# Half of h's last block in one stationary operand: 17 down products for a tile and not 18

## What is computed

```python
def fp4_quant_dequant(x):            # along the last dim, in blocks of 16
    xb = x.reshape(shape[:-1] + (shape[-1] // BLOCK, BLOCK))
    scale = jnp.maximum(jnp.max(jnp.abs(xb), axis=-1, keepdims=True) / 6.0, 1e-12)
    ...                              # round xb / scale to the FP4 grid, times scale
def fp4_linear(x, w):
    return jnp.einsum('bsk,nk->bsn', fp4_quant_dequant(x), fp4_quant_dequant(w))

x = x + xattn(layernorm(x), ctx)     # 16 heads of 64, 154 context rows
xn = layernorm(x)
h = silu(fp4_linear(xn, w_gate)) * fp4_linear(xn, w_up)    # 704 hidden columns
out = x + fp4_linear(h, w_down)                            # 704 -> 256
```

## Time and profile before

| | us |
|---|---|
| median of 3 runs | 885.43 |
| lowest, highest | 885.17, 888.35 |
| the profiled execution | 887.63 |
| its span, first to last instruction | 885.5 |
| TensorE busy in it | 834.0 (94%) |
| VectorE busy | 709.2 (80%) |
| POOL busy | 539.2 (61%) |
| ScalarE busy | 525.7 (59%) |
| mean granted TensorE clock | 0.988 of 2.4 GHz |

### The profile page before, as it was taken

How to read it: one execution, slowest core, us unless ns; L and a number is a source line. 1 busy time by engine, 2 the same in 40 slices (tenths; PEclk the granted TensorE clock), 3 DMA queues, 4 the chain that set the end, 5 groups by cost and what they waited for, 6 DMA issues and landing times.

```text
span 885.5 us, 19161 instructions
## 1 busy us (share of the span) xinstructions
PE 834.0 (94%) x6278; PEld 805.2 (91%) x6278; DVE 709.2 (80%) x2157; ACT 525.7 (59%) x1878; POOL 539.2 (61%) x810
## 2 busy tenths in 40 slices
PE   4887799999999999999999999999999999999986
PEld 4766789999988999999998999999999999999985
DVE  5659788877877888887877888887778788888887
ACT  4555466666665666667565666666666666666531
POOL 6437766765644666675653766665644577666644
PEclk9889999999999999999999999999999999999999
DMA  8101000001010000001000000000100000000000
GB/s 248 37 25 45 1 20 13 24 14 48 8 37 19 13 26 13 26 13 43 13 31 25 7 24 14 24 14 13 50 7 19 13 14 25 14 19 14 7 7 19
DMA packets 20137, 23.14 MB, mean 26 GB/s; under 512 B 2658, under 2 KB 18250, under 8 KB 20042
## 3 DMA queue, kind: packets, MB, share of 16 engines
q1 hardware_dynamic: 20042, 21.94, 8.2%
HBM read 17.74 MB, written 4.19 MB: 25 GB/s over the span
## 4 chain that ended last, share of the span: by engine, by line
PE 81%; DVE 11%; POOL 3%; issue 2%; ACT 2%; DVEq 0%; POOLq 0%; ACTq 0%
PE ps_g L1246 12%; PE ps_s L1203 11%; PE ps_q L1161 10%; PE ps_t L1213 7%; PE ps_o L1226 7%; PE ps_o L1228 7%; PE ps_o L1227 7%; PE ps_g L1124 3%; PE ps_m L1089 3%; PE ps_m L1260 3%; PE ps_m L1262 2%; PE ps_m L1261 2%; PE ps_q L1124 2%; DVE negmax L884 1%; DVE pT_lo L737 1%
## 5 line engine op out<-in xcount | busy, mean ns | idle before, releaser
L511 POOL TENSOR_TENSOR probs<-probs,rsum 128x308 f32<-128x308 f32 x256 | 179.5, 702 | 244.5 <-DVE rsum L848 244.1
L684 ACT ACTIVATE probs<-ps_s,negmax 128x154 f32<-128x154 f32 x512 | 194.7, 386 | 190.2 <-DVE negmax L884 188.4
L884 DVE TENSOR_REDUCE negmax<-ps_s 128x2 f32<-128x308 f32 x256 | 121.1, 473 | 92.5 <-PE ps_s L1203 91.6
L1226 PE MATMUL ps_o<-B_sb,pT_lo 128*128 128x256 f32 x640 | 180.9, 283 | 0.9 <-DVE x_both L939 0.6
L1228 PE MATMUL ps_o<-B_sb,pT_hi 128*128 128x256 f32 x640 | 180.6, 282 | 0.0
L1227 PE MATMUL ps_o<-B_sb,pT_hi 128*128 128x256 f32 x640 | 180.3, 282 | 0.0
L737 DVE TENSOR_TENSOR pT_lo<-ps_t,pT_hi 128x256 fp32r<-128x256 f32 (+1 forms) x256 | 122.9, 480 | 34.4 <-ACT pT_hi L572 34.0
L1246 PE MATMUL ps_g<-WGU,xqT_hi 128*128 128x352 f32 x504 | 131.8, 343 | 2.0 <-DVE B_sb L737 1.7
L1213 PE MATMUL ps_t<-ident,probs 128*128 128x128 f32 x640 | 112.8, 274 | 15.4 <-DVE pT_lo L737 13.2
L1226 PEld LDWEIGHTS ps_o<-B_sb,pT_lo 128*128 128x128 f32 x640 | 121.1, 189 | 1.4 <-issue 0.8
L1228 PEld LDWEIGHTS ps_o<-B_sb,pT_hi 128*128 128x128 f32 x640 | 121.4, 190 | 0.0
(11 more groups left out here) (228 smaller groups left out, 2213.8 us busy)
## 6 DMA issues: line engine op xcount, KB each, us to landing
xa<-in_x_dram SPq DMA_DIRECT2D x33, 128.0 KB, 2.2
xr<-in_x_dram SPq DMA_DIRECT2D x32, 128.0 KB, 2.0
out_dram<-y_xn SPq DMA_DIRECT2D x30, 128.0 KB, 1.7
W_sb<-in_L_xattn_Wk_dram SPq DMA_DIRECT2D x4, 512.0 KB, 4.6
W_sb<-in_L_xattn_Wv_dram SPq DMA_DIRECT2D x3, 512.0 KB, 3.3
probs<-in_L_xattn_Wq_dram SPq DMA_DIRECT2D x2, 512.0 KB, 8.0
Wo_sb<-in_L_xattn_Wo_dram SPq DMA_DIRECT2D x1, 1024.0 KB, 9.2
VT<-in_L_ffn_w_down_dram SPq DMA_DIRECT2D x2, 352.0 KB, 3.9
```

The source lines that it names most:

```text
L511: pool.tensor_tensor(unit, unit, rsum[:, 2 * u:2 * u + 2].unsqueeze(2) .to_broadcast([P, 2, M]), ALU.mult).then_inc(norm_p, 1)
L684: ins = act.activation(probs[:, h, 0:M], ps_s[k % 2][:, s * M:(s + 1) * M], ACT.Exp, bias=negmax[:, h:h + 1], accum_out=sums[:, h:h + 1])
L884: dve.tensor_reduce(negmax[:, 2 * k:2 * k + 2], ps_s[k % 2][:, 0:UM].rearrange("p (h m) -> p h m", h=2), AX_X, ALU.max, negate=True).then_ ...
L1226: pe.matmul(ps_o[:, 0:C], lo[:, j, :], w[:, 0:C], start=first, stop=False)
```

## The change

The last block of h has only 64 rows that aren't zero. The changed kernel puts the low part of this half block below the high part, in partitions 64 to 127 of hqT[0]'s block 5. WD's block 5 gets the weights' half block twice, in partitions 0 to 63 and 64 to 127. Two matmuls with this operand, one with the weights' low part and one with their high part, then give (high + low) x (high + low), where there were three. For that:

- VectorE's hqT_lo of blocks 3 to 5 becomes two operations: blocks 3 and 4 as before into hqT[1] (128x256), and the half block from partitions 0 to 63 into partitions 64 to 127 of hqT[0] (64x128).
- POOL fills the padding of the w_down chunks with the last 64 columns' rounded values and no longer with zeros: a product of 128x64 between the second and third step of `fp4`, on the same queue. The two memsets and the wait for b_mm go, and TensorE's wait for pad_p with them.
- The three tiles in `finish` keep 18 matmuls with low parts of their own; since WD's padding isn't zero any more, VectorE sets tile 31's padding of h to zero.

```diff
+            def round_stage(c, i):
+                n = RAW_N[c]
+                v, scale = raw[RAW_IN[c]], raw_s[c % 2][:, 0:n // BLOCK]
+                if i == 2 and c >= DOWN:
+
+                    pool.wait_ge(raw_p, 3 * c + 2)
+                    pool.tensor_tensor(v[:, F:FP].rearrange("p (b k) -> p b k", k=BLOCK),
+                                       v[:, F - D:F].rearrange("p (b k) -> p b k", k=BLOCK),
+                                       scale[:, (F - D) // BLOCK:].unsqueeze(2).to_broadcast([P, D // BLOCK, BLOCK]),
+                                       ALU.mult).then_inc(pad_p, 1)
+                    pool.wait_ge(pad_p, c - DOWN + 3)
+                fp4(v[:, 0:n], raw_c[c % 2][:, 0:n], scale, raw_p, 3 * c, (raw_v, 6 * c + 6), (i,))
+
             def round_chunk(c):
-                n = RAW_N[c]
-                fp4(raw[RAW_IN[c]][:, 0:n], raw_c[c % 2][:, 0:n], raw_s[c % 2][:, 0:n // BLOCK], raw_p, 3 * c,
-                    (raw_v, 6 * c + 6))
+                for i in range(3):
+                    round_stage(c, i)
...
-                    if isinstance(t, int) and t == 1 and k == 0:
-
-                        pool.wait_ge(b_mm, B_JOBS)
-                        for c in range(DOWN, CHUNKS):
-                            pool.memset(raw[RAW_IN[c]][:, F:FP], 0.0).then_inc(pad_p, 1)
...
                     if down and k in (5, 6):
                         r = k - 5
-                        lo_part(hqT[1][:, 3 * r:3 * r + 3, :], parts(ps_m, 3), hqT[0][:, 3 * r:3 * r + 3, :],
-                                (hqT_hi, 2 * d + r + 1), hqT_lo)
+                        if r == 0:
+                            lo_part(hqT[1][:, 0:3, :], parts(ps_m, 3), hqT[0][:, 0:3, :], (hqT_hi, 2 * d + 1), hqT_lo)
+                        else:
+                            dve.wait_ge(hqT_hi, 2 * d + 2)
+                            dve.tensor_tensor(hqT[1][:, 3:5, :], parts(ps_m, 2), hqT[0][:, 3:5, :].bitcast(F32), ALU.subtract)
+                            dve.tensor_tensor(hqT[0][D:P, 5, :], ps_m[0:D, 2 * P:3 * P], hqT[0][0:D, 5, :].bitcast(F32),
+                                              ALU.subtract).then_inc(hqT_lo, 1)
...
                 weights_lo(T, PAIRS - 1)
+                dve.memset(hnT[:, F:FP], 0.0).then_inc(ppad_v, 1)
...
                 pe.wait_ge(raw_p, 3 * c + 3)
-                if c == DOWN:
-                    pe.wait_ge(pad_p, 4)
...
-                down_terms(ps_m, *hqT, range(FT)).then_inc(d_mm, 1)
+                down_terms(ps_m, *hqT, range(FT - 1))
+
+                for part in range(2):
+                    ins = pe.matmul(ps_m[:, 0:C], hqT[0][:, FT - 1, :], WD[:, FT - 1, part * C:(part + 1) * C],
+                                    start=False, stop=(part == 1))
+                ins.then_inc(d_mm, 1)
...
                     pe.wait_ge(hd_v, 3)
+                    pe.wait_ge(ppad_v, 2)
...
-                down_product(R, (xqT_lo, S + 1))
+                m_free((xqT_lo, S + 1), (y_v, R + 1))
+                pe.wait_ge(hqT_lo, 2 * R + 2)
+                down_terms(ps_m, *hqT, range(FT)).then_inc(d_mm, 1)
```

## The result

The changed kernel takes 891.37 us (median of 6 runs, 889.26 to 893.52). The kernel before, on the same chips, takes 886.50 (6 runs, 884.94 to 888.35). The ratio is 1.0057, with a 95% interval of 1.0040 to 1.0074: the change costs 4.9 us, between 3.5 and 6.6. The forecast was +4.05 us on 885.43, the median of the three runs known then.

The account below looks back on a forecast made before the run. The prediction took both TensorE and VectorE to be on the path in every tile. Its terms, -3.42 + 6.68 + 0.74 + 0.05 = +4.05 us on a median of 885.43, gave 889.5 us, range 884.0 to 892.0.

Parts of the forecast that it names:

- matmul removed: Down product on TensorE, 29 tiles: one matmul less saves 0.118 us each, 3.42 us in all.
- given back behind the matmul: VectorE's stretch from slot 0's negmax: all 3.42 us counted as arriving, since 0.19 of 0.31 us idle time remain.
- VectorE's pair: Slot 6, hqT_lo split in two: both operations held as in K_lo, +0.30 us a tile, +6.68 us in all.
- w_down's preparation: Weight setup on POOL: two 128x64 products of +0.37 us each, on the path, 0.74 us, between 0 and 1.0.
- tail: Last tiles: VectorE gets a memset of 64 columns, 0.05 us, between 0 and 0.1.
- Rival (b): Slot 6: a write into the other half doesn't hold VectorE, +1.39 in place of 6.68, 884.2 us; chance 0.11.
- Rival (c): Slot 6's second operation: moving between partition halves costs more than K_lo's pair, +0.19 us in 23 tiles, 893.9; chance 0.08.
- Rival (a): Whole kernel: busy shares are right and VectorE's extra time is hidden behind TensorE, 882.8 us; chance 0.06.
- What is late next: Slot 7's transposes start 0.30 us later in 12 tiles, 0.28 in 11; in six tiles idle time takes it.
- A steady pair: Two steady tiles, from product to product, now 45.60 us, would take 0.34 us more.
- the warm-up up to tile 3 moves by more than 1 us: Time up to tile 3: named as one sign that the prediction is wrong.
- The prediction's line between same and slower: Whole time: about 0.5% can be told from no change, 889.9 us; same 0.59, slower 0.38.

Follow-up runs that it names:

- e2: Kernel before with 18 down matmuls and only VectorE's split, second operation writing the other partition half: 892.66 us, ratio 1.0080.
- e4: Kernel before with only the change's w_down preparation on POOL and the tail's memset: 886.32 us, ratio 1.0009.
- e8: The changed kernel run once more, nothing altered: 891.18 us, ratio 1.0045 against the kernel before.
- e3: Kernel before with 18 down matmuls and only VectorE's split, second operation writing the same half it reads: 886.37 us, ratio 1.0014.
- e5: Changed kernel with the 64x128 operation moved to slot 7 behind pT_lo, except in five setup steps: 882.20 us, ratio 0.9950 against the kernel before.
- e7: The kernel before run once more, nothing altered: 885.68 us, ratio 0.9995.
- e6: Kernel before with 17 matmuls, VectorE's operation whole, POOL doubling h's half block, ACT copying the high part: 889.09 us, ratio 1.0021.
- e9: Changed kernel with POOL's addition of the output bias moved from slot 0 to slot 5: 889.2 us, run once.
- e10: Kernel before with 17 down matmuls, VectorE's operation whole, POOL's output bias addition moved from slot 0 to 5: 885.2 us, run once.
- e11: e5 with POOL's addition of the output bias moved from slot 0 to slot 5: 881.93 us, ratio 0.9962 against the kernel before.

## The prediction against the runs, point by point

| term | predicted | measured | from |
|---|---|---|---|
| matmul removed, 29 x 0.118 | -3.42 | -3.42 | start to start in the product |
| given back behind the matmul | 0 | about +0.6 | 19 x 0.034 us of hn<-eh,scales; the middle: 3.52 + 3.30 - 22 x 0.28 |
| VectorE's pair | +6.68 | about +6.4 | 23 x 0.28; e2's rows |
| w_down's preparation | +0.74 | +0.73 | e4's front, one execution |
| tail | +0.05 | not told apart | the changed kernel's own two are 40.98 and 41.61 |
| sum | +4.05 | about +4.3 | timed: +4.9 (3.5 to 6.6) |

- **The matmul.** Price and place were right. The step that was wrong is the sentence that the 0.118 us reaches VectorE's next stretch as long as the idle time before negmax isn't used up. That idle time did remain, 0.17 us where the prediction said 0.19:

```profile
325.56 0.48 DVE L896 TENSOR_REDUCE negmax<-ps_s 128x2 f32<-128x308 f32 x1 [0.17 <-PE ps_s L1214]
```

  But a test for idle time before one operation isn't a test for what comes behind it. 0.7 us later VectorE and POOL meet in an operation that a shift of 0.12 us turns into a wait, and in slot 1 TensorE then waits for the q_lo that stands behind it (the q product starts at 329.00, 0.05 us behind q_lo's end, and 0.19 behind the transposes in front of it where it was 0.15). By the durations it cost some 0.6 of the 3.42 us (0.65 in this trace, 0.46 in e8's); what moving the addition gives back is 0.49 in the 14 undisturbed periods.
- **The split.** Both times were taken from K_lo and came out: second start 0.42 to 0.43 us behind the first, 283 to 286 ns long, negmax 0.32 behind. The pair is 0.74 us and not 0.75, the cost 0.28 and not 0.30: priced about 0.3 us too high over all tiles. The open question, whether the output alone holds, is settled by e2 and e3. Rival (b), which would have been 884.2 us, would have needed e3's rows in the changed kernel. Rival (c), that crossing is dearer, falls too.
- **Rival (a), hidden.** The wait of TensorE grew by what the pair grew, 0.28 to 0.30 us, in every one of the 12 tiles with a wait; e5 shows the reverse, the same work behind the pT_lo without a net cost.
- **What is late next.** Three classes of tiles were forecast, +0.30, +0.28 and 0. Measured: the even periods went from 23.16 to 23.36 us, the odd from 22.45 to 22.64 (each holds one split, less 0.12 of matmul, plus 0.04 of POOL), and the six tiles that were to absorb it did (periods of 27.87 us went to 27.76, of 34.01 to 33.88).
- **A steady pair** was to grow by 0.34 us; it grew by 0.41. The pair's 2 x 0.28 is 0.02 less than forecast, POOL's hold is 0.07 more.
- **The front.** That "the warm-up up to tile 3 moves by more than 1 us" was named as what would make the prediction wrong, and it did move, by 2 us in the profiled execution, but not through the change: e7 has the kernel before at 140.15 where it was at 142.44. So the condition was badly chosen: it can't tell the change from the scatter of single executions. Closer are executions whose stretches at 1.2 GHz stand at the same places (e4 and e8 against before), and these too only to some tenths: e5, with the same preparation, has its first product at 143.75.
- **The size.** The forecast of 889.5 us lay 0.46% above the kernel before, the measurement lies 0.57% above (0.40% to 0.74%). Of the 1.9 us between 889.5 and 891.37, 1.1 are the kernel before itself, 886.50 in six runs after 885.43 in three; the other 0.8 lie within the interval. The terms give about 4.3, and in part they come so near by luck: the pair was priced 0.3 us too high and the give-back 0.6 too low. The prediction's line between same and slower, 0.5%, runs through the measured interval, so it doesn't say on which side the change lies; that it costs time is clear.

## What to carry to other kernels

Price an edit at the place where its engine is waited for, and not by that engine's share: 0.28 us of VectorE per tile cost 6 us in front of the pT_lo that TensorE waits for and had no net cost behind it. When a saving moves one engine against another, look through the next stretch for operations of both that would now overlap, not only for the idle time in front of it. A slot to which an operation is moved must be free in every step, the setup steps too, and for the other engine that meets what is pushed back there.

## What the hardware showed that was not expected

- A write to the other half of the partitions, the inputs unchanged, holds VectorE twice: 0.74 us in place of 0.53 for the same two operations (e2, e3).
- VectorE's operation with two inputs in SBUF ends some 748 ns after POOL's addition if that one is still running 0.14 us after its start, and isn't touched if it ends sooner: 882 to 886 ns with 132 ns of overlap (e5), 890 with 142 (e6), 925 with 177 (the changed kernel).
- A memset on POOL, which only writes, holds VectorE's 16-column tensor_scalar on one SBUF input until it ends: 0.74 to 0.75 us in place of 0.17 (e9, e10, e11).
- Two executions of one kernel differ by up to 2.9 us before the first down product (the changed kernel: 140.42 and 143.34; before: 142.44 and 140.15), in the main by where and for how long TensorE's clock stands at 1.2 GHz in the warm-up, and by 0.1 us in the 700 us behind it.
